# The tail of a batch moved to other slots, VectorE's order in a slot, and where padding rows are zeroed

## The chip, the core and the metric

One core of a Trainium2 chip runs the whole program. The metric is the device time of one execution in microseconds (us). TensorE multiplies matrices into PSUM. VectorE and ScalarE read PSUM and compute, GpSimd computes on SBUF only, and SP (SyncE) issues DMAs. Each engine works through its own queue in order and waits on semaphores that the others raise.

## The reference, cut to what matters

Sixteen sequences (B = 16) of 112 rows and 256 features pass through four layers, each with a residual and a tanh gate:

```python
x = x + tanh(g_xattn[0]) * L0_xattn(layernorm(x), ctx)   # 16 heads of 64, 375 context rows
x = x + tanh(g_ffn[0])   * L0_ffn(layernorm(x))          # fft, one 256x256 product, ifft: one matrix in the end
x = x + tanh(g_xattn[1]) * L1_xattn(layernorm(x), ctx)   # one head of 256
x = x + tanh(g_ffn[1])   * L1_ffn(layernorm(x))          # 16 experts, the best 4 of each row
```

The last layer sends each row to its four best experts out of 16. An expert computes `y = swiglu(t @ w1 + b1) @ w2 + b2`, and the four results are summed with softmax weights.

## The kernel before, in words

**Slots.** Time is cut into slots (`g`). Batch b's attention takes slots 16b to 16b+15, and every engine runs one loop over the slots from -10 to 295. `due(g, at)` gives the batch whose step `at` falls into slot g. Three batches overlap in a slot: the attention of batch b (heads in 8 pairs p: scores S in slot 2p, transposition PT in 2p+3, product O in 2p+4), the first projections of batch b+1 (negative places), and the tail of batch b-1 (places 20 to 45). A period is 16 slots. Below, slots are counted modulo 16.

**Projections.** `KV_AT` lists (kind, number, place): "x" transposes the normed rows, "q", "k" and "v" are the projections, "c" transposes the context, "r" and "e" belong to the router. They share two PSUM banks in turn (`KV`). Use n+2 of a bank waits until ScalarE has copied the high half of use n and VectorE has subtracted it to get the low half. VectorE does that in the slot after (`kv_groups(g - 1)`).

**The tail.** After the first layer's out projection (T0A, step 0) it is a chain through one PSUM bank `TL`: step 1 transposes the normed rows n1, 2 is the fft layer's matrix, 3 transposes n2, 4 makes the query of the second attention (results qk_hi, qk_lo), 5 its scores, 6 transposes prob1, 7 and 8 are the products with context and value matrix, 9 transposes the normed rows tn, 10 is the router. `T_EARLY` and `T_LATE` give the slot of each on TensorE, in front of or behind that slot's projections. Step n waits until the reader of step n-1 is done (`TL_READ`). GpSimd computes the power -0.5 of the variance and VectorE refines it (`refine`, two small steps from SBUF to SBUF).

**Order in a slot.** TensorE: S or PT, early tail step, projections, late tail step, O. VectorE: low halves of the slot before, `tail`, negmax of S, rinv, `ahead` (norm of the next batch: AT_LN, AT_XN), pT_lo, `tail_end`. ScalarE: oT, `tail`, the two exponentials of S or pT_hi, high halves of the projections, `tail_end`. GpSimd: `tail`, the multiplication of prob by rinv, `tail_end`, the scatters.

**Experts.** Each expert has a region of 1920 rows in DRAM (`rows_by_expert`). Slots 41 to 44 of a batch scatter its rows there, one choice each. 72 tiles of 128 rows are then computed: 34 (N_A) planned after batch 13, 22 (N_B) planned after batch 15, and 16 (N_P), one for each expert's last, partly filled tile. The order is A, four of B, the 16 P, the rest of B. SP loads them into six buffers, each with a register load of the start row and a DMA (lines 664 to 674), and waits ahead of tile 34 (k = N_A) until the last batch's rows have landed. Rows behind an expert's last row must be zero, so ScalarE's queue issues 16 DMAs in slots 8 to 38 of batch 0 that write zeros over all 16 regions (1920 KB each). The first scatter waits for them.

Of the kernel before, what the change touches and what calls it, by code (L numbers as in the profile page):

```python
# [272 lines left out]
def program(nc, sb, event, sem, banks, ident, acc, earlier, ones, seen, sel, tile_f, wkv, stage_w, tile_bufs,  # L273
# [5 lines left out]
    with scope:  # L279
# [197 lines left out]
        KV_AT = (("k", 2, 0), ("v", 2, 1), ("k", 3, 3), ("q", 1, 4), ("k", 4, 5), ("v", 3, 6),  # L477
# [53 lines left out]
        AT_SPLIT = (-2, 1, -1, 3)  # L531
# [166 lines left out]
        def _(eng):  # L698
# [40 lines left out]
            def tail(g):  # L739

                tb = due(g, 20)
                if tb:
# [147 lines left out]
        def _(eng):  # L890
# [56 lines left out]
            def tail(g):  # L947

                tb = due(g, 27)
# [121 lines left out]
        def _(eng):  # L1071
# [126 lines left out]
            def tail(g):  # L1198
# [5 lines left out]
                tb = due(g, 23)  # L1204
                if tb:

                    e_tl.wait_ge(eng, tb, 3)
                    e_xb.wait_ge(eng, tb, 1)
                    e_tl_dve.done(eng.scalar_tensor_tensor(x2[:, :], TL[0:TQ, 0:D], gt[0:TQ, 2:3],
                                                           xb1[:, :], ALU.mult, ALU.add))  # L1210
                    e_tl_dve.wait_ge(eng, tb, TL_READ[2][1])
                    stats(ct, x2[:, :], ln_t)
                    e_mv_t.done(eng.tensor_scalar(ln_t[:, 8:9], ln_t[:, 7:8], EPS, None, ALU.add))
                tb = due(g, 27)
                if tb:

                    e_tl.wait_ge(eng, tb, 6)
                    e_tl_dve.done(eng.tensor_reduce(sm1[:, 1:2], TL[0:TQ, 0:SK], AX.X, ALU.max))
                    e_tl_dve.wait_ge(eng, tb, TL_READ[5][1])
                    ct(eng.tensor_tensor(sm1[:, 2:3], sm1[:, 1:2], sm1[:, 0:1], ALU.add))  # L1220
                    ct.wait_ge()
                    e_bias1.done(eng.tensor_tensor(sm1[:, 3:4], sm1[:, 0:1], sm1[:, 2:3],
                                                   ALU.subtract))
                tb = due(g, 31)
                if tb:
# [11 lines left out]
                                                ALU.subtract, ALU.mult))  # L1237

            def tail_end(g):
# [17 lines left out]
                if tb:
# [652 lines left out]
```

## Time and profile before

| | |
|---|---|
| median of 3 runs | 1160.99 us (1158.84 to 1163.97) |
| profiled execution | 1161.57 us, span from first to last instruction 1159.8 us, mean granted clock 0.984 |
| TensorE matmul | 1075.9 us busy, 93% |
| VectorE, ScalarE, GpSimd | 773.1 us (67%), 631.4 us (54%), 519.8 us (45%) |
| DMA | 95.82 MB, of which the 16 zero fills are 30.7 MB |
| chain that ended last | TensorE 61%, VectorE 16%, ScalarE 10% of the span |

Busy shares are means over the whole span. The stages differ: the first batch (to about 90 us) has loads and set-up, from 134 us on the periods are alike, from about 915 us the last tail and the expert tiles run, and after 1120 us the results are gathered. In rows TensorE is PE (its weight loads PEld), VectorE is DVE, ScalarE is ACT, GpSimd is POOL. A start time is counted from the span's start; a matmul's end is modelled and overlaps the next one's start.

### The profile page before, as it was taken

The numbers are of one execution on the slowest core, as the hardware profiler recorded it, in microseconds if no ns is written. First come the engines' busy times: TensorE is split into PE (matmuls) and PEld (weight loads), VectorE is DVE, ScalarE is ACT, GpSimd is POOL, SyncE is SP. The second block draws the span as 40 slices with busy tenths as digits, with TensorE's granted clock in tenths as the row PEclk, the third lists the DMA queues.
The fourth block names the chain that finished last, engine by engine and source line by source line (L and its number), as shares of the span: only waits on it lengthen the run. The fifth ranks groups of instructions, "written<-read, shape, count | busy, mean of one in ns | idle before, by whom it ended". The sixth has DMA issues, their size and how long they took to land.

```text
span 1159.8 us, 22342 instructions
## 1 busy us (share of the span) xinstructions
PE 1075.9 (93%) x7361; PEld 930.8 (80%) x7361; DVE 773.1 (67%) x1963; ACT 631.4 (54%) x1676; POOL 519.8 (45%) x745
## 2 busy tenths in 40 slices
PE   3889999999999999999999999999999779899995
PEld 3688888888888888888788888888887668789983
DVE  2544677767676767776676777676766665686665
ACT  2533556555656565655556565656564545555650
POOL 3512345453535454454535354536354404565441
PEclk9989999999999999999999999999999888999998
DMA  5395882010101011010001010101000522234469
GB/s 150 96 329 207 309 297 63 5 34 9 30 27 31 27 31 35 23 35 22 23 16 32 8 38 9 31 9 31 5 18 9 176 83 78 99 108 152 133 198 287
DMA packets 82382, 95.82 MB, mean 83 GB/s; under 512 B 9291, under 2 KB 74445, under 8 KB 82272
## 3 DMA queue, kind: packets, MB, share of 16 engines
q1 hardware_dynamic: 41904, 44.94, 13.5%
q10 hardware_dynamic: 31520, 32.51, 7.9%
q0 software_dynamic: 8848, 16.96, 4.2%
q8 instruction: 63, 1.03, 0.4%
q14 instruction: 47, 0.39, 0.1%
HBM read 41.98 MB, written 52.39 MB: 81 GB/s over the span
## 4 chain that ended last, share of the span: by engine, by line
PE 61%; DVE 16%; ACT 10%; issue 6%; DMA 4%; POOL 3%; SPq 1%; DVEq 0%; ACTq 0%; POOLq 0%
PE ps_kv L1568 14%; PE ps_ot L1854 8%; PE ps_ot L1668 5%; PE ps_kv L1650 5%; PE ps_s L1811 5%; PE ps_pt L1821 5%; ACT prob L938 4%; DVE negmax L1467 3%; PE ps_pt L1780 3%; PE ps_ot L1793 3%; DVE pT_lo L1478 2%; DVE k_lo L1152 2%; ACT v_hi L928 2%; DMA zb<-places 2%; PE ps_ot L1712 2%
## 5 line engine op out<-in xcount | busy, mean ns | idle before, releaser
L855 POOL TENSOR_TENSOR prob<-prob,rinv 112x750 f32<-112x750 f32 x128 | 185.4, 1448 | 310.7 <-DVE rinv L1472 310.4
L938 ACT ACTIVATE prob<-ps_s,negmax 112x375 f32<-112x375 f32 x256 | 144.7, 570 | 236.4 <-DVE negmax L1467 236.4
L1478 DVE TENSOR_TENSOR pT_lo<-ps_pt,pT_hi 125x672 fp32r<-125x672 f32 x128 | 109.7, 857 | 77.0 <-ACT pT_hi L1051 77.0
L1568 PE MATMUL ps_kv<-ctxT_hi,wkv 128*128 128x376 f32 x512 | 141.6, 357 | 7.8 <-DVE v_lo L1156 3.8
L1467 DVE TENSOR_REDUCE negmax<-ps_s 112x2 f32<-112x750 f32 x128 | 119.0, 930 | 0.1
L1156 DVE TENSOR_TENSOR v_lo<-ps_kv,v_hi 125x512 fp32r<-125x512 f32 x96 | 66.4, 692 | 77.2 <-ACT v_hi L928 77.2
L1568 PE MATMUL ps_kv<-wkv,ctxT_hi 128*125 128x512 f32 x384 | 112.2, 414 | 3.6 <-DVE n_e L1116 2.3
L1821 PE MATMUL ps_pt<-ident,prob 112*125 112x112 f32 x768 | 104.9, 273 | 1.3 <-POOL prob L855 1.3
L814 POOL DMA_INDIRECT places<-ysb,place_i x72 | 70.3, 976 | 69.1 <-ACT ysb L1010 55.9
L1051 ACT ACTIVATE pT_hi<-ps_pt 125x672 fp32r<-125x672 f32 x128 | 93.5, 730 | 9.0 <-PE ps_pt L1821 1.0
L1821 PEld LDWEIGHTS ps_pt<-ident,prob 112*125 112x125 f32 x768 | 95.1, 191 | 1.7 <-POOL prob L855 1.7
L1568 PEld LDWEIGHTS ps_kv<-ctxT_hi,wkv 128*128 128x128 f32 x512 | 85.8, 191 | 11.0 <-ACT xnT L911 6.0
L1039 ACT ACTIVATE oT<-ps_ot 64x112 f32<-64x112 f32 x256 | 65.9, 257 | 51.8 <-PE ps_ot L1854 48.6
L1152 DVE TENSOR_TENSOR k_lo<-ps_kv,k_hi 128x376 fp32r<-128x376 f32 x128 | 69.6, 544 | 30.9 <-ACT k_hi L926 30.2
L1568 PEld LDWEIGHTS ps_kv<-wkv,ctxT_hi 128*125 128x125 f32 x384 | 66.4, 187 | 25.6 <-issue 10.0
L1428 DVE TENSOR_TENSOR tT_lo<-ps_s,tT_hi 128x512 fp32r<-128x512 f32 (+1 forms) x76 | 50.3, 662 | 47.9 <-ACT tT_hi L998 47.8
L1854 PE MATMUL ps_ot<-pT_hi,v_hi 125*128 125x224 f32 x384 | 72.6, 298 | 3.1 <-issue 3.0
L928 ACT ACTIVATE v_hi<-ps_kv 125x512 fp32r<-125x512 f32 x96 | 57.4, 598 | 32.3 <-PE ps_kv L1568 32.3
L926 ACT ACTIVATE k_hi<-ps_kv 128x376 fp32r<-128x376 f32 x128 | 61.9, 484 | 20.9 <-PE ps_kv L1568 20.7
L792 POOL DMA_INDIRECT entries<-entry,at x64 | 61.5, 962 | 18.9 <-issue 14.6
L796 POOL DMA_INDIRECT rows_by_expert<-row,at x64 | 60.1, 940 | 19.5 <-issue 19.2
L1854 PEld LDWEIGHTS ps_ot<-pT_hi,v_hi 125*128 125x128 f32 x384 | 58.0, 193 | 12.9 <-issue 9.7
(298 smaller groups left out, 2623.8 us busy)
## 6 DMA issues: line engine op xcount, KB each, us to landing
rows_by_expert<-stage_w ACTq DMA_DIRECT2D x16, 1920.0 KB, 7.3
xg<-rows_by_expert SPq DMA_DIRECT2D x72, 128.0 KB, 2.1
zb<-places SPq DMA_DIRECT2D x16, 448.0 KB, 15.0
arena<-in_L_ffn_mlp_w SPq DMA_DIRECT2D x24, 256.0 KB, 4.4
ctx_in<-in_ctx SPq DMA_DIRECT2D x16, 375.0 KB
acc<-in_L_xattn_w_kv SPq DMA_DIRECT2D x4, 512.0 KB, 13.1
stage_w<-in_L_ffn_mlp_w SPq DMA_DIRECT2D x8, 256.0 KB, 3.0
x_in<-in_x SPq DMA_DIRECT2D x16, 112.0 KB, 2.1
```

The lines of the kernel that those rows point to most:

```text
L814: eng.indirect_dma_start(places[:, :], bass.IndirectOffsetOnAxis(place_i[:, n:n + 1], 0), ysb[:, j % YB, :], None).then_inc(f_z[j % YB], 16)
L855: e_prob.done(eng.tensor_tensor(prob[0:TQ, p % 2, :, :], prob[0:TQ, p % 2, :, :], rinv[:, 2 * p:2 * p + 2].unsqueeze(2).broadcast_to([TQ, ...
L928: ins = eng.activation(v_hi[0:KEYT, n % NKEY, n // NKEY * 512:(n // NKEY + 1) * 512], bank[0:KEYT, :], ACT.Copy)
L938: e_exp.done(eng.activation(prob[0:TQ, p % 2, half, :], S[0:TQ, half, 0:SK], ACT.Exp, bias=negmax[:, h:h + 1], accum_out=rowsum[:, h:h + 1]))
L1051: e_pt_hi.done(eng.activation(pT_hi[:, :, :, :].rearrange("p h k t -> p h (k t)"), PT[0:KEYT, :, 0:NKEY * TQ], ACT.Copy))
L1152: ins = eng.tensor_tensor(k_lo[:, n, :], bank[:, 0:SKE], k_hi[:, n, :].bitcast(F32), ALU.subtract)
L1156: ins = eng.tensor_tensor(v_lo[0:KEYT, n % NKEY, at], bank[0:KEYT, :], v_hi[0:KEYT, n % NKEY, at].bitcast(F32), ALU.subtract)
L1467: e_max.done(eng.tensor_reduce(negmax[:, 2 * p:2 * p + 2], S[0:TQ, :, 0:SK], AX.X, ALU.max, negate=True))
L1478: e_pt_lo.done(eng.tensor_tensor(pT_lo[:, :, :, :].rearrange("p h k t -> p h (k t)"), PT[0:KEYT, :, 0:NKEY * TQ], pT_hi[:, :, :, :].bitcas ...
L1568: last = eng.matmul(out_, lhs(i, k), rhs(j, k), start=(n == 1), stop=(n == KT * len(PASSES)))
L1821: last = eng.transpose(PT[0:KEYT, half, k * TQ:(k + 1) * TQ], prob[0:TQ, p % 2, half, k * KEYT:(k + 1) * KEYT], ident[0:TQ, 0:TQ])
L1854: last = eng.matmul(OT[:, 0:2 * TQ].rearrange("p (h t) -> p h t", t=TQ), vv[i][0:KEYT, k, p * 128:(p + 1) * 128], pT[j][:, :, k, :], start ...
```

## The change

Three things are changed.

1. Places. The tail's steps 1 to 5 move from the end of slots 21, 22, 24, 25, 26 to the front of 22, 23, 25, 26, 27; steps 6 and 7 from the front of 28 and 29 to their end. The steps of the other engines follow. Of the projections, k2 goes from slot 0 to 1, v2 from 1 to 2, q1 from 4 to 5 (behind k4), q0 of the next batch from 14 to 11, c1 from 13 to 12, k0 from 14 to 13, k1 from 15 to 14. AT_XN goes from slot 7 to 9.
2. VectorE calls `tail` behind negmax, rinv and `ahead` instead of ahead of them. x2 and the second attention's maximum move from `tail` to `tail_end`, n2 moves from `tail_end` of slot 23 to `tail` of 24, and the router's ranking moves to `tail` (places 34 and 35). On GpSimd xb1 moves behind the multiplication. A projection two uses behind an "r" now waits for VectorE's half of it too.
3. Padding. The 16 zero fills and the waits for them go. VectorE's plan of batch 15 computes each expert's first row behind its last (`pad_i`), and SP, behind the loads of tiles 30 to 33, copies 128 zero rows to there from a spare tile in DRAM, four experts behind each load. The load of tile 38 waits for all of them.

```diff
-        KV_AT = (("k", 2, 0), ("v", 2, 1), ("k", 3, 3), ("q", 1, 4), ("k", 4, 5), ("v", 3, 6),
+        KV_AT = (("k", 2, 1), ("v", 2, 2), ("k", 3, 3), ("k", 4, 5), ("q", 1, 5), ("v", 3, 6),
                  ("k", 5, 7), ("v", 4, 8), ("k", 6, 9), ("v", 5, 10), ("k", 7, 11), ("x", 0, -6),
-                 ("c", 0, -4), ("c", 1, -3), ("q", 0, -2), ("k", 0, -2), ("k", 1, -1), ("v", 0, -1),
+                 ("q", 0, -5), ("c", 0, -4), ("c", 1, -4), ("k", 0, -3), ("k", 1, -2), ("v", 0, -1),
                  ("v", 1, 0), ("r", 0, 36), ("e", 0, 38))
...
-        AT_LN, AT_XN, AT_XB0 = -10, -9, 6
-        T_EARLY = {20: 0, 28: 6, 29: 7, 30: 8, 32: 9, 33: 10}
-        T_LATE = {21: 1, 22: 2, 24: 3, 25: 4, 26: 5}
+        AT_LN, AT_XN, AT_XB0 = -10, -7, 6
+        T_EARLY = {20: 0, 22: 1, 23: 2, 25: 3, 26: 4, 27: 5, 30: 8, 32: 9, 33: 10}
+        T_LATE = {28: 6, 29: 7}
...
-        AT_SPLIT = (-2, 1, -1, 3)
+        AT_SPLIT = (-3, 1, -1, 3)
...
+        PAD_AT = tuple(range(N_A - 4, N_A))
...
+                if k == N_A + B_FIRST:
+                    eng.wait_ge(f_zero, 16 * NE)
                 c_turn.wait_ge(eng, k - XB + 1)
...
+                if k in PAD_AT:
+                    eng.wait_ge(s_pad, 1)
+                    first = PAD_AT.index(k) * NE // len(PAD_AT)
+                    for e in range(first, first + NE // len(PAD_AT)):
+                        end = eng.value_load(pad_i[0:1, e:e + 1], min_val=0, max_val=NE * REGION - TILE)
+                        eng.dma_start(rows_by_expert[bass.ds(end, TILE), :],
+                                      rows_by_expert[NONE * TILE:(NONE + 1) * TILE, :]).then_inc(f_zero, 16)
...
-                if g in AT_ZERO:
-
-                    if g == AT_ZERO[0]:
-                        eng.wait_ge(s_fill, 2)
-                    e = AT_ZERO.index(g)
-                    eng.dma_start(rows_by_expert[e * REGION:(e + 1) * REGION, :].rearrange("(p n) d -> p n d", p=128),
-                                  zeros.unsqueeze(1).broadcast_to([128, REGION // 128, D])).then_inc(f_zero, 16)
...
+                    if not early:
+                        ct(eng.tensor_tensor(todo[:, :], n_e[:, :], region[:, :], ALU.add))
+                        ct.wait_ge()
+                        eng.tensor_copy(pad_i[:, :], todo[:, :]).then_inc(s_pad, 1)
...
                 for step, kind, n in kv_groups(g - 1):
                     projection(step, kind, n)
-                tail(g)
...
                 ahead(g)
+                tail(g)
...
-                    if KV_ORDER[use - 2][0] not in "xr" or kind == "w":
+                    if KV_ORDER[use - 2][0] != "x":
                         eng.wait_ge(kv_dve, KV_LO[use - 1])
```

## Rows read from the trace of the kernel before

**Rows 1.** stages; columns: time, us, busy PE, PEld, DVE, ACT, POOL, clock, DMA, GB/s

```profile
134.20:188.91 54.71, 53.84 (x367) 45.74 (x367) 38.66 (x101) 31.63 (x89) 22.75 (x27) 1.00 0.68 237
790.76:845.47 54.71, 53.72 (x367) 45.68 (x367) 38.65 (x101) 31.53 (x89) 26.59 (x32) 1.00 0.07 19
```

**Rows 2.** timeline of PEld: start, us, line, operation, [idle before <- releaser]

```profile
574.89 0.41 PEld L1854 LDWEIGHTS ps_ot<-pT_hi,v_hi 125*128 125x128 f32 x3 [0.42 <-issue]
616.48 0.20 PEld L1687 LDWEIGHTS ps_ot<-ident,n12t 112*128 112x128 f32 x2 [0.87 <-issue]
619.71 0.47 PEld L1695 LDWEIGHTS ps_ot<-qbk,nT 128*112 128x112 f32 x4 [0.42 <-ACT nT L944]
626.59 0.30 PEld L1568 LDWEIGHTS ps_kv<-ctxT_hi,wkv 128*128 128x128 f32 x2 [0.35 <-ACT xnT L911]
```

**Rows 3.** timeline of DVE, slots 7 and 8

```profile
614.58 0.63 DVE L1170 SCALAR_TENSOR_TENSOR ln_t<-ln_t 112x1 f32<-112x1 f32 x1
616.74 0.93 DVE L1467 TENSOR_REDUCE negmax<-ps_s 112x2 f32<-112x750 f32 x1
```

**Rows 4.** timeline of ACT, slot 8

```profile
617.70 0.57 ACT L938 ACTIVATE prob<-ps_s,negmax 112x375 f32<-112x375 f32 x1 [3.42 <-DVE negmax L1467]
```

**Rows 5.** timeline of PE, slots 10 and 11: x, O, PT

```profile
623.38 0.36 PE L1603 MATMUL ps_kv<-ident,xn 112*128 112x112 f32 x2
624.61 0.49 PE L1854 MATMUL ps_ot<-pT_hi,v_hi 125*128 125x224 f32 x3
625.61 0.81 PE L1821 MATMUL ps_pt<-ident,prob 112*125 112x112 f32 x6
```

**Rows 6.** timeline of ACT, slots 9 and 10

```profile
621.29 0.60 ACT L989 ACTIVATE qk_hi<-ps_ot,kbq 128x112 fp32r<-128x112 f32 x2
625.56 0.79 ACT L911 ACTIVATE xnT<-ps_kv,cols 128x112 f32<-128x112 f32 x2
```

**Rows 7.** timeline of DVE, slot 9

```profile
622.07 0.57 DVE L1262 SCALAR_TENSOR_TENSOR qk_lo<-ps_ot,kbq,qk_hi 128x112 fp32r<-128x112 f32 x2
```

**Rows 8.** timeline of POOL, slot 7

```profile
613.66 1.54 POOL L855 TENSOR_TENSOR prob<-prob,rinv 112x750 f32<-112x750 f32 x1
```

**Rows 9.** timeline of all engines, batch 0, slot 7

```profile
51.65 1.44 POOL L855 TENSOR_TENSOR prob<-prob,rinv 112x750 f32<-112x750 f32 x1 [0.26 <-DVE rinv L1472]
51.72 1.38 DVE L1172 SCALAR_TENSOR_TENSOR ln_h<-ln_h 112x1 f32<-112x1 f32 x1
```

**Rows 10.** timeline of all engines, slot 12

```profile
573.11 0.42 PE L1811 MATMUL ps_s<-k_hi,q_hi 64*112 64x376 f32 x2
577.85 0.55 DVE L1143 TENSOR_TENSOR ctxT_lo<-ps_kv,ctxT_hi 128x375 fp32r<-128x375 f32 x1 [1.47 <-ACT ctxT_hi L920]
```

**Rows 11.** timeline of PE, head

```profile
16.28 3.72 PE L1650 MATMUL ps_kv<-xnT,wq 128*128 128x112 f32 x16 [0.24 <-DVE ctxT_lo L1143]
69.14 0.54 PE L1643 MATMUL ps_kv<-ident,ctx_in 125*128 125x125 f32 x3 [1.45 <-DMA ctx_in<-in_ctx]
```

**Rows 12.** stages of the head, columns as in rows 1

```profile
70.00:75.00 5.00, 5.00 (x28) 4.95 (x28) 1.74 (x10) 0.84 (x3) 0.00 (x1) 0.55 0.98 350
75.00:80.00 5.00, 5.00 (x35) 4.42 (x34) 2.16 (x3) 2.11 (x6) 1.43 (x1) 0.76 0.75 260
```

**Rows 13.** timeline of SP's DMA issues, tiles 33, 34 and 41

```profile
1030.28 0.34 SPq L674 DMA_DIRECT2D xg<-rows_by_expert  x1
...
1044.24 0.34 SPq L674 DMA_DIRECT2D xg<-rows_by_expert  x1
...
1052.46 0.34 SPq L674 DMA_DIRECT2D xg<-rows_by_expert  x1
```

**Rows 14.** timeline of DVE, first step of the last plan

```profile
1026.02 0.42 DVE L1341 TENSOR_REDUCE full<-cmp_b 112x16 f32<-112x256 f32 x1
```

**Rows 15.** timeline of PE, tile 34

```profile
1046.33 0.44 PE L1767 MATMUL ps_s<-ident,xg 128*128 128x128 f32 x2 [1.52 <-DMA xg<-rows_by_expert]
```

More of the change, by code:

```diff
@@ L744, in tail @@
                     e_rs_t.done(eng.tensor_tensor(ln_t[:, 9:10], ln_t[:, 8:9], consts[0:TQ, 0:1], ALU.pow))
-                    e_xb.done(eng.tensor_tensor(xb1[:, :], x1[:, :], rows[0:TQ, 1, :], ALU.add))
-                tb = due(g, 23)
+                tb = due(g, 24)
                 if tb:
@@ L756, in tail_end @@
             def tail_end(g):
-                tb = due(g, 23)
+                tb = due(g, 21)
+                if tb:
+                    e_xb.done(eng.tensor_tensor(xb1[:, :], x1[:, :], rows[0:TQ, 1, :], ALU.add))
+                tb = due(g, 24)
                 if tb:
@@ L977, in tail_end @@
             def tail_end(g):
-                tb = due(g, 21)
+                tb = due(g, 22)
                 if tb:
                     normed(tb, 1)
-                tb = due(g, 24)
+                tb = due(g, 25)
                 if tb:
                     normed(tb, 3)
-                tb = due(g, 25)
+                tb = due(g, 26)
                 if tb:
@@ L1203, in tail @@
                     normed(tb, 0)
-                tb = due(g, 23)
+                tb = due(g, 24)
                 if tb:
[L1207 to L1223, printed above, removed]
+                    e_rs_t.wait_ge(eng, tb, 2)
+                    normed(tb, 1)
                 tb = due(g, 31)
@@ L1237, in tail @@
                                                 ALU.subtract, ALU.mult))
+                tb = due(g, 34)
+                if tb:
+                    ct.wait_ge()
+                    ct(eng.tensor_tensor(cmp_b[:, :, :], cmp_b[:, :, :], earlier[0:TQ, :, :], ALU.mult))
+                    ct.wait_ge()
+                    ct(eng.tensor_tensor(cmp_a[:, :, :], cmp_a[:, :, :], cmp_b[:, :, :], ALU.add))
+                    ct.wait_ge()
+                    ct(eng.tensor_reduce(rk[:, 0, :], cmp_a[:, :, :], AX.X, ALU.add))
+                    ct.wait_ge()
+                    e_seen.wait_ge(eng, tb, 0)
+                    e_mask.done(eng.tensor_scalar(mask[:, :], rk[:, 0, :], TOPK - 0.5, None, ALU.is_lt))
+                tb = due(g, 35)
+                if tb:
+                    e_gexp.wait_ge(eng, tb, 1)
+                    ct(eng.scalar_tensor_tensor(rk[:, 3, :], rk[:, 0, :], TOPK - 0.5, rk[:, 1, :],
+                                                ALU.is_lt, ALU.mult, accum_out=rs[:, 1:2]))
+                    ct.wait_ge()
+                    ct(eng.reciprocal(rs[:, 2:3], rs[:, 1:2]))
+                    ct.wait_ge()
+                    e_route.done(eng.tensor_scalar(route[:, :], rk[:, 3, :], rs[:, 2:3],
+                                                   gt[0:TQ, 3:4], ALU.mult, ALU.mult))
             def tail_end(g):
@@ L1253, in tail_end @@
                 if tb:
-                    e_rs_t.wait_ge(eng, tb, 2)
-                    normed(tb, 1)
-                tb = due(g, 25)
+                    e_tl.wait_ge(eng, tb, 3)
+                    e_xb.wait_ge(eng, tb, 1)
+                    e_tl_dve.done(eng.scalar_tensor_tensor(x2[:, :], TL[0:TQ, 0:D], gt[0:TQ, 2:3],
+                                                           xb1[:, :], ALU.mult, ALU.add))
+                    e_tl_dve.wait_ge(eng, tb, TL_READ[2][1])
+                    stats(ct, x2[:, :], ln_t)
+                    e_mv_t.done(eng.tensor_scalar(ln_t[:, 8:9], ln_t[:, 7:8], EPS, None, ALU.add))
+                tb = due(g, 26)
                 if tb:
@@ L1265, in tail_end @@
                     e_tl_dve.done(last)
+                tb = due(g, 27)
+                if tb:
+                    e_tl.wait_ge(eng, tb, 6)
+                    e_tl_dve.done(eng.tensor_reduce(sm1[:, 1:2], TL[0:TQ, 0:SK], AX.X, ALU.max))
+                    e_tl_dve.wait_ge(eng, tb, TL_READ[5][1])
+                    ct(eng.tensor_tensor(sm1[:, 2:3], sm1[:, 1:2], sm1[:, 0:1], ALU.add))
+                    ct.wait_ge()
+                    e_bias1.done(eng.tensor_tensor(sm1[:, 3:4], sm1[:, 0:1], sm1[:, 2:3],
+                                                   ALU.subtract))
                 tb = due(g, 28)
```

37 lines of the change are left out of this document (9 added, 28 removed).

## The prediction

> **What bounds the kernel now.** I read the stage table first. The steady stretch, in which one batch's attention, the batch before's tail and the next batch's first projections share 16 slots, takes 54.71 us a batch with TensorE busy 53.7 at clock 1.00. It takes that both while the zero fill moves 237 GB/s and when only 19 GB/s flow [rows 1]. So TensorE's queue is the bound there, and the zero fill already costs nothing after batch 1. What an order change can win is TensorE's waits. The weight-load row, which shows the start of each group of matmuls, has four real ones in a period: the O product on pT_lo (0.42), tail step 3 on n2 (0.87), step 4 on the copy nT (0.42), k7 on v5's low half and xnT (0.35) [rows 2]. Then I followed VectorE, ScalarE and GpSimd through slots 7 to 12, since those waits come from there: slots 7 to 9 hold nearly all of VectorE's small tail work, so negmax of slot 8 starts at 616.74 and ScalarE's exponentials have waited 3.42 us for it [rows 3, 4].
>
> Fourteen periods (batches 1 to 14) carry tail and next batch together, so 1 us a period is 14 us. The profiled execution took 1161.57 us, 0.6 above the median of the runs, and the sum is made against it.
>
> **The spread, part by part.** By my count of PE work, the fullest slots of before (4, 0 and 14) lose q and k projections to slots 5, 11, 13 and 14. The work is the same; only waits can change.
>
> *What goes.* Step 3 moves from the end of slot 8 to the front of slot 9, and n2 now comes before the choice block and after a negmax that is earlier: its 0.87 goes. k7 stands behind step 5 in slot 11, so v5's low half has time: 0.35 goes. The second-layer exponential moves from slot 11 to slot 12 on ScalarE, so pT_hi of slot 11 no longer queues behind it: 0.42 goes. Step 4 still follows step 3 by one ScalarE copy that queues behind the exponentials: its 0.42 stays. Gone: 0.87 + 0.42 + 0.35 = 1.6 us a period.
>
> *What comes, slot 11.* Step 4 now runs in slot 10 ahead of v5 and x, and ScalarE takes its result (qk_hi) only after the exponentials of slot 10, v5's copy and the two xnT copies; VectorE's qk_lo follows, and step 5 stands in TensorE's queue right behind O and PT. In before, x started at 623.38 on TensorE and xnT ended at 625.56 + 0.79 = 626.35, 2.97 later, because the exponentials had waited for a late negmax [rows 5, 6]. With that lag, step 5 could start 2.97 + qk_hi 0.60 + qk_lo 0.57 + about 0.3 of handoffs = 4.4 us after x; TensorE's own work until then is x 0.12 (to the next start), O 1.00 and PT 0.58 = 1.7 [rows 5 to 7]. Upper bound of the wait 2.7. Lower bound, with ScalarE idle when x ends: the later of v_hi and xnT leaves about 1.1, then 0.60, 0.57 and 0.3, against 1.6 of work: 0.95. Between them the state of VectorE decides. In slot 9 it now has rinv, then the refinement for xn, then pT_lo, then k6's low half and the negmax of slot 10. rinv releases GpSimd's 1.44 us multiply of prob, and the refinement reads two SBUF tensors: at 51.72 exactly this sequence held the second refinement step for 1.38 us, until 53.10, where GpSimd's multiply from 51.65 ended (53.09); at 614.58 a step held 0.63, to the end of the multiply of 613.66 [rows 3, 8, 9]. In before's steady slot 7 the xn refinement escaped, because GpSimd first did a small power there. In slot 9 there is none. So negmax of slot 10 comes about 3.4 us behind its S, ScalarE's exponentials end about when x has been done for a microsecond, and the wait comes out near 2.2. I take 2.2, by the row at 51.72, which is the same instruction sequence.
>
> The Trainium skill (SBUF — State Buffer, Who interferes with whom) states that a VectorE instruction with two SBUF inputs and a GpSimd instruction that reads SBUF exclude each other, and that the later one blocks for the whole of the other. The trace agrees in the 1.38 us above.
>
> *What comes, slots 12 and 13.* c0 and c1 stand together in slot 12 and k0 in slot 13, where before they had slots 12, 13 and the end of 14. c1 needs the bank that q0 (end of slot 11) leaves, and k0 needs c1's low half. ScalarE copies c only after the exponentials of slot 12. In before S of slot 12 started at 573.11 and c0's low half ended at 577.85 + 0.55 = 578.40, 5.3 us later [rows 10]; a second c adds about 0.45. TensorE's own work from S to k0 is now S 0.69, two c 0.82, step 6 0.42, O 1.02 and PT 0.58 = 3.5 (start-to-start distances of the same period). With before's lag, the wait is 5.75 - 3.5 = 2.2. VectorE is less behind here (q0's low half, then negmax at once): S to negmax 1.4 with q0 in front, negmax 0.96, exponentials 1.11, two copies 0.8, low half and handoffs 0.9 = 5.1: wait 1.6. With negmax prompt it is 0.6 less and c1's own bank wait is still there: 1.0, or 0.6 if that falls too. I take 1.6, bounds 0.6 and 2.2.
>
> Sum: 2.2 + 1.6 - 1.6 = +2.2 us a period, 14 x 2.2 = **+31 us**. Bounds: 0.95 + 0.6 - 1.6 = 0 and 2.7 + 2.2 - 1.6 = +3.3, so 0 to +46.
>
> **VectorE's order in a slot** puts negmax ahead of the tail; that is inside the above (slot 8's negmax about 1.4 us earlier). **TensorE's extra wait** for VectorE's half of r sits before q1 in slot 5, behind k4; VectorE does r's 0.17 first in its slot, so S's and PT's 1.3 us cover it; uncovered it is 0.2 a period. Cost 0.
>
> **Head.** At the start q0 (3.72 us there) goes ahead of both c, and xn is two slots later in program order only. k0 must wait for c, which waited for q0: bounds 0 and +3.7, taken +2, since TensorE waits elsewhere in the first slots [rows 11]. Without the zero fill the batch-1 context load need not share 350 GB/s: TensorE waited 1.45 us for it, and then its granted clock was 0.55 in 70 to 75 us and 0.76 in 75 to 80, means between the levels 1.2 GHz (0.5) and 2.4 GHz (1.0), which is 2.2 + 1.2 us of full-speed work [rows 11, 12]. Bounds 0 and -4.9; taken -3. Head together **-1**.
>
> **Padding.** 16 copies now stand in SP's queue between the loads of tiles 30 to 33 and tile 34, each a register load and a DMA. SP's loads ran 7 steps in 8.22 us when nothing held them, 1.17 each [rows 13]. They may begin when VectorE's first plan step is done, 1026.02 + 0.42 + about 0.5 = 1027.0 [rows 14]. Sixteen copies, three loads and tile 34's own then end at about 1028 + 19 x 1.12 to 1.17 = 1049 to 1050. Before, tile 34 was issued at 1044.24, held by the last scatter, and TensorE waited for it to 1046.33 [rows 13, 15]; after it the tiles follow back to back, so nothing behind it gives time back. Tile 33 (1030.28 before) goes to about 1044 and is late too, inside the same delay. Cost **+5**. Bounds: 0 (SP does not mind, or the scatter ends later), +9 (0.2 more per copy, and loads landing behind copies of the same queue). The wait for all copies at tile 38 comes four loads later and is covered by six buffers.
>
> **The rest.** Two VectorE steps in the plan, about 0.4 us; ScalarE's 16 DMA issues go, and ScalarE is no bound. The last batch's tail alone runs steps up to one slot later, while the scatter stays in slots 41 to 44: 0, give or take 3.
>
> Total 1161.6 + 31 - 1 + 5 = 1196.6; less the 0.6 by which the profiled run lies above the median: **1196**.
>
> **Rivals.** (a) *VectorE's reductions first pay, faster.* Place: ScalarE's queue in slots 10 and 12. If negmax is prompt enough that the two new waits stay under 1.6 - 4/14 = 1.3 us together, the change wins; with none at all it wins 1.6 x 14 = 22: 1161 - 22 + 4 = 1143. For it: the 3.42 us that ScalarE waited. Against: even an idle ScalarE leaves 0.95 + 0.6. Chance 0.06. (b) *The gate in slot 9 stays open*: GpSimd starts late, xn is not held; step 5 waits 1.0, so +1.0 a period, +14 + 4: 1179. Chance 0.22. (c) *Every such VectorE step behind rinv is held.* In slot 5 the refinement for n1 now meets the multiply and the xb1 add that was moved behind it, and in slot 15 the third step before tn; pT_lo and k4's low half in slot 5 come up to 2 us later, and v3 in slot 6 waits 0.4 to 1.1: 14 x 0.75 = 10 more, 1206. By the skill's rule above it is this. Chance 0.15. (d) *New waits equal the old*, with the copies hidden or the head's gain paying for them: 1158 to 1165. Chance 0.07. My forecast, 1186 to 1203, has 0.50.
>
> **From these the numbers.** A measurement here can tell 0.5% (5.8 us). Faster 0.06, same 0.07, slower 0.87. The range leaves out (a), (d) and the top of (c): 1170 to 1212.
>
> **What would show it.** Period: 56.5 to 57.5 between the same slot of two batches (55.7 under b, 53.1 under a). TensorE's row: the 0.87 before step 3 gone, some 2 us before step 5's first matmul with qk_lo as releaser, some 1.2 before k0 with the low half of c. VectorE: the xn refinement of 1.3 us or so in each period. SP: 16 DMA issues about 1.1 us apart and tile 34 at 1049. Clock 1.00 in 70 to 80 us. I am wrong if step 5 or k0 start without a wait, or if SP issues the copies in much less.

## The result and the profile after

The changed kernel takes 1233.54 us (median of 4 runs, 1233.13 to 1236.98) where the kernel before takes 1162.48 beside it: a ratio of 1.062, 95% interval 1.059 to 1.066. It is slower, by 71 us and not by the 35 that were forecast (31 - 1 + 5), and beyond the upper end of the forecast, 1212. The profiled execution took 1233.86 us with a span of 1232.0 and a mean granted clock of 0.960.

Where the 72.3 us between the two profiled executions arise, by four marks that both traces have (the first transposition of xn of batch 2 and of the last batch, the plan step `full` of the last plan, tile 34's load):

| stretch | before | after | more |
|---|---|---|---|
| start to x of batch 2 | 130.97 | 138.25 | 7.3 |
| 13 periods, to x of the last batch | 711.25 | 755.23 | 44.0 |
| last period and last tail, to `full` | 183.80 | 199.20 | 15.4 |
| `full` to tile 34's load | 18.22 | 26.23 | 8.0 |
| rest | | | -2.4 |

A second pair of traces, x1 and x2 below, gives 8.0, 44.1, 7.7, 8.4 and 1.4 by the same marks. The last tail's 15.4 and the rest do not repeat, the other three do.

The timeline of TensorE after, at the new place of step 5 in slot 11 (the three products onto `ps_ot`), and k7 behind it (`ps_kv`), in two batches that follow each other. Columns: start, us, engine, line, operation, [idle before <- releaser].

```profile
488.02 0.36 PE L1614 MATMUL ps_kv<-ident,xn 112*128 112x112 f32 x2
...
545.26 0.36 PE L1614 MATMUL ps_kv<-ident,xn 112*128 112x112 f32 x2
...
549.31 0.76 PE L1579 MATMUL ps_ot<-ctxT_hi,qk_hi 128*112 128x376 f32 x2 [2.03 <-DVE qk_lo L1279]
...
551.12 0.83 PE L1579 MATMUL ps_kv<-ctxT_hi,wkv 128*128 128x376 f32 x2
551.75 0.83 PE L1579 MATMUL ps_kv<-ctxT_lo,wkv 128*128 128x376 f32 x2
...
604.08 0.36 PE L1614 MATMUL ps_kv<-ident,xn 112*128 112x112 f32 x2
...
608.12 0.58 PE L1579 MATMUL ps_ot<-ctxT_hi,qk_hi 128*112 128x376 f32 x2 [2.02 <-DVE qk_lo L1279]
...
609.22 0.51 PE L1579 MATMUL ps_kv<-ctxT_hi,wkv 128*128 128x376 f32 x2
609.56 0.50 PE L1579 MATMUL ps_kv<-ctxT_lo,wkv 128*128 128x376 f32 x2
```

Both batches wait 2.0 us for qk_lo, as forecast. Behind the wait the same pairs of products start 0.63 us apart in the first batch and 0.34 in the second. The stages of these stretches (time, us, busy PE, PEld, DVE, ACT, POOL, clock, DMA, GB/s) say why:

```profile
549.30:551.20 1.90, 1.89 (x7) 1.85 (x8) 1.29 (x3) 0.26 (x1) 1.28 (x1) 0.56 0.00 0
551.20:553.10 1.90, 1.90 (x9) 1.90 (x8) 0.87 (x3) 0.00 (x0) 1.44 (x3) 0.54 0.01 0
...
608.00:610.00 2.00, 1.89 (x11) 1.92 (x12) 1.94 (x4) 0.37 (x1) 1.27 (x1) 1.00 0.00 0
610.00:612.00 2.00, 2.00 (x19) 2.00 (x17) 0.88 (x3) 0.48 (x1) 1.54 (x3) 1.00 0.01 0
```

In the first batch TensorE's granted clock is at 1.2 GHz (0.5; the slices take in a bit of either side) for step 5 and k7, in the next it stays at 2.4 GHz. So periods of 57.25 and 58.80 us take turns through the whole steady stretch (x at 488.02, 545.26, 604.08), against 54.71 [rows 1]. The 2.0 us come from where the forecast had them. VectorE, GpSimd and ScalarE after, slots 9 and 10, and VectorE in slot 5:

```profile
541.52 1.44 POOL L866 TENSOR_TENSOR prob<-prob,rinv 112x750 f32<-112x750 f32 x1 [2.71 <-DVE rinv L1482]
541.59 1.38 DVE L1176 SCALAR_TENSOR_TENSOR ln_h<-ln_h 112x1 f32<-112x1 f32 x1
544.60 0.92 DVE L1477 TENSOR_REDUCE negmax<-ps_s 112x2 f32<-112x750 f32 x1
545.55 0.57 ACT L949 ACTIVATE prob<-ps_s,negmax 112x375 f32<-112x375 f32 x1 [3.13 <-DVE negmax L1477]
547.80 0.62 ACT L1000 ACTIVATE qk_hi<-ps_ot,kbq 128x112 fp32r<-128x112 f32 x2
548.60 0.57 DVE L1279 SCALAR_TENSOR_TENSOR qk_lo<-ps_ot,kbq,qk_hi 128x112 fp32r<-128x112 f32 x2
...
585.41 1.38 DVE L1174 SCALAR_TENSOR_TENSOR ln_t<-ln_t 112x1 f32<-112x1 f32 x1 [0.19 <-POOL ln_t L754]
```

The refinement's second step for xn lasts 1.38 us, to 542.97, where GpSimd's multiply ends (542.96), exactly as in [rows 9]. The median of its 16 executions is 1380 ns. negmax of slot 10 then starts 2.2 us behind the end of S, ScalarE idles 3.13 us, and qk_hi stands behind all of it. The other waits, on TensorE and its weight loads (PEld): step 4, c0, c1, k0, step 3 and the projection v3:

```profile
542.48 0.47 PEld L1706 LDWEIGHTS ps_ot<-qbk,nT 128*112 128x112 f32 x4 [0.45 <-ACT nT L955]
...
555.53 0.31 PEld L1654 LDWEIGHTS ps_kv<-ident,ctx_in 125*128 125x128 f32 x3 [0.25 <-issue]
556.37 0.51 PE L1654 MATMUL ps_kv<-ident,ctx_in 125*128 125x125 f32 x3 [0.29 <-DVE q_lo L1151]
559.86 0.62 PE L1579 MATMUL ps_kv<-ctxT_hi,wkv 128*128 128x376 f32 x2 [1.00 <-DVE ctxT_lo L1147]
...
588.76 0.20 PEld L1698 LDWEIGHTS ps_ot<-ident,n12t 112*128 112x128 f32 x2 [0.26 <-issue]
589.26 0.75 PEld L1579 LDWEIGHTS ps_kv<-wkv,ctxT_hi 128*125 128x125 f32 x4 [0.30 <-issue]
```

Step 3's 0.87 of [rows 2] has become 0.26, k7's 0.35 and O's 0.42 are gone, step 4's stays. Last, the plan step on VectorE and SP's issues behind it (L676 loads a tile, L683 is a zero copy, four in a group):

```profile
1092.68 0.42 DVE L1347 TENSOR_REDUCE full<-cmp_b 112x16 f32<-112x256 f32 x1
1094.33 4.61 SPq L683 DMA_DIRECT2D rows_by_expert<-rows_by_expert  x4
1099.69 0.35 SPq L676 DMA_DIRECT2D xg<-rows_by_expert  x1
...
1112.47 0.35 SPq L676 DMA_DIRECT2D xg<-rows_by_expert  x1
1113.64 4.43 SPq L683 DMA_DIRECT2D rows_by_expert<-rows_by_expert  x4
1118.91 1.48 SPq L676 DMA_DIRECT2D xg<-rows_by_expert  x2
...
1121.03 0.44 PE L1778 MATMUL ps_s<-ident,xg 128*128 128x128 f32 x2 [1.94 <-DMA xg<-rows_by_expert]
```

Four copies and a load take 6.4 us (1112.47 to 1118.91), 1.3 a DMA, and TensorE stands 1.94 us for tile 34.

### The profile page after: what moved, and what is told of

The parts are those of the page before. It is cut to its first block and busy times, and to the rows that moved or that the text cites. A ratio compares the mean times of both kernels' runs of the same rounds, so it can differ in the third digit from the quotient of the medians.

```text
span 1232.0 us, 22439 instructions
## 1 busy us (share of the span) xinstructions
PE 1102.4 (89%) x7361; PEld 958.5 (78%) x7361; DVE 833.2 (68%) x1965; ACT 627.7 (51%) x1676; POOL 518.6 (42%) x745
## 3 DMA queue, kind: packets, MB, share of 16 engines
q10 hardware_dynamic: 544, 1.05, 0.3%
## 5 line engine op out<-in xcount | busy, mean ns | idle before, releaser
L1579 PE MATMUL ps_kv<-ctxT_hi,wkv 128*128 128x376 f32 x512 | 149.4, 375 | 18.6 <-DVE ctxT_lo L1147 17.7
L1579 PE MATMUL ps_kv<-wkv,ctxT_hi 128*125 128x512 f32 x384 | 115.4, 423 | 6.2 <-DVE wkv L1459 2.8
L1579 PEld LDWEIGHTS ps_kv<-ctxT_hi,wkv 128*128 128x128 f32 x512 | 94.6, 202 | 23.9 <-DVE ctxT_lo L1147 20.5
L1865 PE MATMUL ps_ot<-pT_hi,v_hi 125*128 125x224 f32 x384 | 69.7, 291 | 2.1 <-DVE pT_lo L1489 2.1
L1579 PE MATMUL ps_kv<-ctxT_lo,wkv 128*128 128x376 f32 x256 | 68.3, 350 | 0.0
L1661 PEld LDWEIGHTS ps_kv<-xnT,wq 128*128 128x128 f32 x512 | 65.7, 202 | 2.6 <-ACT xnT L922 2.6
```

What stands on the lines that cost most here:

```text
L1579: last = eng.matmul(out_, lhs(i, k), rhs(j, k), start=(n == 1), stop=(n == KT * len(PASSES)))
L1661: last = eng.matmul(bank[:, a * TQ:(a + 1) * TQ], wq[:, k, p * 128:(p + 1) * 128], xnT[:, k, :], start=(k == 0), stop=(k == KT - 1))
L1865: last = eng.matmul(OT[:, 0:2 * TQ].rearrange("p (h t) -> p h t", t=TQ), vv[i][0:KEYT, k, p * 128:(p + 1) * 128], pT[j][:, :, k, :], start ...
```

## The experiments

Times are medians. A ratio is to the kernel before beside the run, 1162.6 us for u1 to u4 and 1163.5 for u5 to u8. Differences from the changed kernel are to its 1233.5 above.

**u1: the hold.** VectorE's `ahead` in front of rinv:

```diff
+                ahead(g)
+                for p in range(NP):
                     st = due(g, AT_S[p] + 1)     # rinv
...
-                ahead(g)
                 tail(g)
```

> The changed kernel, with VectorE's `ahead` (the refinement for xn) moved in front of rinv in each slot, nothing else. Theory H (GpSimd's multiply, released by rinv, holds the refinement for 1.38 us, so the negmax of slot 10 and all behind it come late): the refinement takes its plain 0.16, negmax of slot 10 comes 1.4 us earlier, the wait before step 5 falls from 2.0 to about 0.8, and the half-rate stretch behind it goes too (0.78 a period on average). 14 x (1.2 + 0.78) = 28 less: 1205 us. Rival (ScalarE's own chain, v5's copy, xnT, qk_hi, sets step 5, whatever VectorE does): the wait stays above 1.6 and the time at 1225 to 1233.

Measured: 1200.07 us, ratio 1.032 (1.030 to 1.035). VectorE in slots 9 and 10 and TensorE at step 5:

```profile
524.29 0.16 DVE L1176 SCALAR_TENSOR_TENSOR ln_h<-ln_h 112x1 f32<-112x1 f32 x1
526.10 0.93 DVE L1477 TENSOR_REDUCE negmax<-ps_s 112x2 f32<-112x750 f32 x1
...
530.88 0.57 PE L1580 MATMUL ps_ot<-ctxT_hi,qk_hi 128*112 128x376 f32 x2 [0.83 <-DVE qk_lo L1279]
```

The step takes 0.16, the wait 0.83, every period 56.05 to 56.09, and none has a slow stretch. Moving three small instructions (the two of the refinement and xn) past one is worth 33 us. Theory H holds.

**u2: step 5 behind k7 and q0.**

```diff
-        T_LATE = {28: 6, 29: 7}
+        T_LATE = {27: 5, 28: 6, 29: 7}
...
                 for at in T_EARLY:
                     tb = due(g, at)
-                    if tb:
+                    if tb and (at != 27 or tb.off >= B - 2):
...
                 for at in T_LATE:
                     tb = due(g, at)
-                    if tb:
+                    if tb and (at != 27 or tb.off < B - 2):
```

> The changed kernel, with step 5 behind slot 11's projections k7 and q0 (except for the tails of the last two batches). Theory A (step 5 is only too early in TensorE's queue): 1.1 us of k7 and 1.9 of q0 cover its wait; wait and half-rate stretch go, 13 x 2.8 = 36 less: about 1197 us. Rival B (the whole slot is late): k7 needs the bank of v5, whose low half VectorE computes behind qk_lo and which ended at 549.76, after step 5 had started; then k7 takes over the wait, 2.0 to 2.5 us, with the half-rate stretch behind it, and the time stays at 1230 to 1242.

Measured: 1272.61 us, ratio 1.096 (1.091 to 1.101), worse than both expected. k7 after this edit, in TensorE's timeline, and then the stage behind it:

```profile
567.46 0.96 PE L1579 MATMUL ps_kv<-ctxT_hi,wkv 128*128 128x376 f32 x2 [2.62 <-DVE v_lo L1160]
```

```profile
568.00:570.00 2.00, 2.00 (x9) 2.00 (x8) 0.14 (x1) 0.29 (x1) 1.84 (x2) 0.50 0.00 0
```

Rival B is right about the mechanism: the whole slot is late, and k7 takes the wait over. It is longer (2.62), and the clock now falls in every period of the middle (61.4 us each), for k7 and all of q0. That was not in the 1242.

**u3 and u5: does the wait bring the clock down?** Products with unused results are put into the wait, 15 and then 10:

```diff
+                st = due(g, AT_S[5] + 1)
+                if st and due(g, 27):
+                    e_exp.wait_ge(eng, st, 12)
+                    for _ in range(15):             # u5: 10
+                        eng.matmul(S[0:TQ, 0, 384:496], ident[0:TQ, 0:TQ], ident[0:TQ, 0:TQ], start=True, stop=True)
                 for at in T_EARLY:
```

> The changed kernel with 15 products of the identity with itself (112 columns each, about 0.12 us each, results unused) put into the 2.0 us wait before step 5. Theory C (the wait is what takes TensorE's clock down to 1.2 GHz in every second period, at 1.55 us each): the granted clock stays 1.00 behind step 5, every period takes 57.25, 7 x 1.55 = 11 less although there is more work: 1222 us. Rival (the clock falls by itself every 116 us or for the load as a whole): periods alternate as before, 1233 us, or more if the products delay step 5.

> As u3_filler, with 10 products instead of 15. In u3_filler each took two instructions and 15 of them 2.88 us, 0.85 more than the wait, so that every period took 57.97, none of them with a half-rate stretch. Ten take 1.92 us and fit into the wait. Theory C (the wait brings the clock down): every period 57.25, and 7 x 1.55 = 11 less than the changed kernel, 1222 us. Rival (the products only bought their own excess): periods of 57.3 and 58.8 by turns, 1233 us.

Measured: u3 1236.67 us (ratio 1.063, 1.058 to 1.067), u5 1221.93 (1.050, 1.047 to 1.054). u3 looks like the rival, but its periods are all 57.95 to 57.98: no alternation, and 0.7 of excess filler in each. In u5 they are 57.24 to 57.32. u5's slot 11, TensorE's timeline and then the stages:

```profile
539.49 2.13 PE L1840 MATMUL ps_s<-ident 112*112 112x112 f32 x20
541.67 0.57 PE L1579 MATMUL ps_ot<-ctxT_hi,qk_hi 128*112 128x376 f32 x2
```

```profile
541.30:543.20 1.90, 1.84 (x13) 1.69 (x12) 1.88 (x5) 0.63 (x1) 0.92 (x1) 1.00 0.01 2
543.20:545.10 1.90, 1.90 (x17) 1.90 (x16) 1.17 (x4) 0.48 (x1) 1.49 (x2) 1.00 0.00 0
```

TensorE does more work and the kernel is 11.6 us faster than the changed one: the half rate came from standing still. Theory C holds, with its size (1222).

**u4: the padding.** The old zero fills and waits come back into the changed kernel, the `if k in PAD_AT` block on SP and `pad_i` go.

> The changed kernel with the old padding (16 zero fills of whole regions on ScalarE's queue, the first scatter waits for them; none on SP). By the trace (16 copies at about 1.3 us each on SP ahead of tile 34): tile 34's load comes 7.6 us sooner after the plan, 1226 us. By the prediction's terms (copies +5, zero fill -3 in the head): 2 less, 1231 us. Rival (tile 34 is late for another reason, and only the head feels the zero fill): 1233 to 1238 us.

Measured: 1222.80 us, ratio 1.051 (1.047 to 1.056), so the new padding costs 10.7 (8.8 between the two profiled executions, and 7.9 of these behind `full`: 131.4 us to the end instead of 139.3). x of batch 2 starts at 137.63 instead of 138.25: in this order of work the zero fill makes no difference to the head, so the prediction's gain there is not to be had. The rival is out. (The 16 zero fills are 31.5 MB, not the 30.7 of the table above: queue q10, which carries them, moves 32.51 MB before and 1.05 MB in v4.)

**u6: c1 and k0 back in slots 13 and 14**, on top of u1:

```diff
-                 ("q", 0, -5), ("c", 0, -4), ("c", 1, -4), ("k", 0, -3), ("k", 1, -2), ("v", 0, -1),
+                 ("q", 0, -5), ("c", 0, -4), ("c", 1, -3), ("k", 0, -2), ("k", 1, -2), ("v", 0, -1),
```

> u1_xn_before_rinv with c1 back in slot 13 and k0 back in slot 14 (ahead of k1), where they were before. Theory K (c1 and k0 stand too close behind the context's copies): their waits of 0.30 and 1.00 us go, 14 x 1.3 = 18 less than u1's 1200: 1182 us. Rival (the waits move on to k1 or to S of slot 16, since ScalarE and VectorE have as much to do as before): 1195 to 1202 us.

Measured: 1197.40 us, ratio 1.030 (1.027 to 1.034), 2.7 less than u1. From TensorE's waits in 440 to 870 us (line <- releaser: us, times, longest):

```profile
PE ps_ot L1724 <- ACT prob1T L968: 6.8, 7, 1.0
```

k0's wait is gone and step 7 has one of the same length: in slot 13 only c1 (0.5 us) stands in front of it now, where k0 stood. The rival holds in time and kind, though the wait moved to step 7 and not to k1 or S.

**u7: the head.** Slots -6 to -1 of batch 0 in the old order, and the first weight split in slot -2:

```diff
+            head = (("x", 0, -6), ("c", 0, -4), ("c", 1, -3), ("q", 0, -2), ("k", 0, -2), ("k", 1, -1), ("v", 0, -1))
-            own = [(due(slot, at), kind, n) for kind, n, at in KV_AT]
+            own = [(due(slot, at), kind, n) for kind, n, at in (KV_AT if slot >= 0 else head)]
```

> The changed kernel, with batch 0's own first projections (slots -6 to -1) in the old order c0, c1, q0, k0, k1, v0 and the first weight split in slot -2; from slot 0 on as changed. Theory L (q0 ahead of c in the first batch, when nothing else covers the copies of c, makes k0 and all behind it late, and this is the head's whole loss): x of batch 2 starts at about 131 instead of 138.25, 7 less: 1226 us. The prediction's term for it was 2 us: 1231. Rival (the loss comes from the other places, k2 and v2 one slot later, in batch 0's slots 0 to 15): 1233.

Measured: 1226.56 us, ratio 1.054 (1.051 to 1.058): 7.0 less. x of batch 2 starts at 132.98, 5.3 earlier and not 7, so theory L holds for 5.3 of the head's 7.3; the 2.0 that are left could be the rival's. In the changed kernel's head TensorE waits 3.69 for c's low half before k0, 2.78 for a weight half before v0, 2.08 and 2.27 in the first O and PT, and its clock falls in 50 to 60 us (0.77) as well as in 80 to 90 (0.66). Which of these carries how much was not separated.

**u8: qk_hi in front of the exponentials**, on top of u1: ScalarE's block for place 26 moves from `tail_end` to `tail`.

> u1_xn_before_rinv with ScalarE's qk_hi taken in front of slot 10's exponentials instead of behind v5's and xn's copies. Theory Q (step 5 waits for its place in ScalarE's queue, not for work): ScalarE is idle there while it waits for negmax, step 5's remaining 0.83 us goes: 14 x 0.83 = 12 less than u1's 1200, 1188 us. Rival (the exponentials start late behind it, and c1, k0 or O wait that much more): 1197 to 1206 us.

Measured: 1182.64 us, ratio 1.017 (1.014 to 1.021), 17.4 less than u1, more than theory Q's 12. Periods are 55.0; TensorE's waits in 440 to 870 us are these two:

```profile
PE ps_kv L1580 <- DVE ctxT_lo L1147: 8.0, 8, 1.0
PE ps_kv L1655 <- DVE q_lo L1151: 2.3, 8, 0.3
```

**The last runs**, v and w, ran where the kernel before takes 1200 us (1199.6 beside v1 to v4, 1200.3 beside w1 to w4), so only their ratios compare. x1, the kernel before again, and x2 ran where it takes 1161. So x1 gave no trace of the 1200, and what made the difference is open. v4's trace shows one part of it, in slot 13 from 190 us on: ScalarE stands 1.97 us, though the product it copies (PE, L1719) is over at 584.1:

```profile
582.62 1.50 PE L1719 MATMUL ps_ot<-prob1T,ctx_in 125*128 125x112 f32 x12
586.10 0.36 ACT L971 ACTIVATE nT<-ps_ot 128x224 f32<-128x224 f32 x1 [1.97 <-remote]
```

Its periods are 56.1 with matmuls as busy as in [rows 1] (53.75) and the clock at 1.00. In v1, v2, w1 and w2 ScalarE has such gaps of up to 1.6, 1.7, 2.3 and 1.5 us at other places of the steady stretch. v3, w3 and w4 have none there, but some of up to 3.8, 5.0 and 3.8 us in the last tail and the expert tiles. The twelve traces from the other places have no ScalarE gap with this releaser at all. Behind `full`, too, all eight runs are some 10 us longer than there, whatever the kernel: 141 to 146 us to the end with the old fills (v2, v3, w1, w4) against 130 to 134 (before, x1, u4), and 152 to 153 with the new padding (v1, v4, w2, w3) against 139 to 144. Since the gaps do not lie alike in all kernels, a ratio here may favour one kernel over another.

**v1, v2, w1, w2: all that was found, together.** u8 with c ahead of q0; v1 and v2 have c0, c1 in slot 12, w1 and w2 c1 in slot 13 with q0; v2 and w1 have the old zero fills:

```diff
-                 ("q", 0, -5), ("c", 0, -4), ("c", 1, -4), ("k", 0, -3), ("k", 1, -2), ("v", 0, -1),
+                 ("c", 0, -4), ("c", 1, -4), ("q", 0, -3), ("k", 0, -2), ("k", 1, -1), ("v", 0, -1),   # w: c1 at -3
```

> u8_qk_hi_early (xn in front of rinv, qk_hi in front of the exponentials) with the next batch's first projections as c0, c1 in slot 12, q0 in 13, k0 in 14, k1 and v0 in 15, and the first weight split in slot -2; so the head too has c ahead of q0. The new padding stays. Theory (the waits of c1 and k0 and the head's q0 are the rest of the loss outside the padding; 1.9 us of q0 in slot 13 cover the copies of c and prob1T's, which took over in u6): 14 x 1.3 = 18 and 5 in the head less than u8's 1183: 1160 us. Rival (a new wait takes their place, as in u6): 1172 to 1180.

> v1_all_waits with the old zero fills instead of the copies on SP's queue. By u4 against the changed kernel (10.7 us): 1150 us if v1 takes 1160, which is below the kernel before (1162). Rival (tile 34 is no longer what the end waits for when the rest is earlier): as v1.

> The changed kernel with all that the runs point to: xn in front of rinv, qk_hi in front of the exponentials, c0 in slot 12, c1 and q0 in 13, k0 in 14, k1 and v0 in 15, and the old zero fills. Theory (the waits named were the loss, and the change's gone waits of 1.6 us a period are a real gain): a period of about 54.0, 0.7 less than before's 54.70; 14 x 0.7 = 10 less, some 5 more in the last tail: 1157 us where the kernel before takes 1162, a ratio of 0.995. Rival (a new wait takes their place): a period of 55 or more and a ratio over 1.005.

> w1_c1_13_old_fill with the new padding (copies on SP's queue, no zero fills). By u4 and v2: 8 to 11 more than w1, a ratio to the kernel before of 1.003 to 1.005. Rival (the copies are hidden once the rest is early): as w1.

Measured: v1 1202.50 us, ratio 1.002 (1.000 to 1.005); v2 1194.23, 0.994 (0.992 to 0.996); w1 1193.54, 0.994 (0.992 to 0.996); w2 1201.18, 1.001 (0.998 to 1.003). v1's theory asked for 0.998 and v2's for 0.990; the rivals (1.008 and more for v1, no difference for v2) are out. So with the waits taken out and the old fills, the new places are 0.6% faster there than the kernel before, and the new padding takes it back (8.3 and 7.6 us). How much of the 0.6% is left where the kernel before takes 1161 was not measured. The period ahead of ScalarE's gaps is 54.51 to 54.54 in all four runs against 54.70 before [rows 1] (54.68 in v4): 14 x 0.17 = 2 us, or 0.2%, is an estimate from these. w1 doesn't reach the period of 54.0: 54.54 before the gaps begin, 55.15 after (56.6 to 56.9 in three). In w2's waits in 406 to 850 us the next one stands in line:

```profile
PE ps_ot L1719 <- ACT prob L970: 7.3, 8, 0.9
```

Step 6 now waits 0.9 for the second layer's exponential. The rival is half right.

**v4: the new padding alone**, put into the kernel before.

> The kernel before with the new padding alone (no zero fills, 16 copies on SP's queue ahead of tile 34, two more VectorE steps). By the changed kernel's trace (copies at about 1.3 us each, tile 34 8.0 us later behind the plan step) and u4, where the zero fill did not move the head: 8 to 10 more, 1171 us. By the prediction's terms (+5 on SP's queue, -3 in the head, where the context load need not share the DMA engines): 2 more, 1165 us. Rival (nothing changes, since tile 34 waits for the last scatter): 1162.

Measured: 1204.38 us, ratio 1.004 (1.002 to 1.006), 4.8 more, between the two sums. x of batch 2 starts at 126.99 (130.97 in the trace of before): with before's order the head seems to gain without the zero fill, as the prediction had it, though the two traces are of the two kinds of place. Pairs from one place say the same with less: with c ahead of q0, x of batch 2 starts at 130.11 without the fill and 132.77 with it (v1, v2), and at 131.65 and 132.89 (w2, w1), where the same kernel differs by up to 0.9 (before, x1).

**v3 and w4: the order alone; w3: the rest without it.** v3 and w4 are the kernel before with `tail(g)` moved behind `ahead(g)`, w3 is the changed kernel with it moved back.

> The kernel before with one part of the change alone: VectorE calls `tail` behind negmax, rinv and `ahead`; all places as before. Theory O (a maximum taken early lets ScalarE start its exponentials early, and that pays by itself): the 3.42 us of ScalarE's wait in slot 8 shrinks and TensorE's 0.42 and 0.35 go, 14 x 0.5 = 7 less: 1155 us. Rival (x2 of place 23 then waits for rinv, and n2 with it, so step 3's wait of 0.87 grows by a microsecond or more): 14 x 1 = 14 more, 1176 us.

> As v3_order_alone: the kernel before with VectorE's `tail` behind negmax, rinv and `ahead`, nothing else. In v3 every period took 57.4, 2.7 more than before's 54.70 where nothing disturbs it, with 1.4 before step 3 and 0.9 before step 6. If that is the order's own price: 14 x 2.7 = 38 and some 4 in the last tail, 1204 us, a ratio of 1.035. If v3 was only caught by what disturbed the kernel before too: a ratio of 1.01 to 1.02.

> The changed kernel with VectorE's `tail` ahead of negmax again, as before the change; places, the steps in `tail` and `tail_end`, and the padding as changed. Theory (the refinement behind rinv in slot 9 and the queue of ScalarE make the loss, and the order of VectorE's queue in the even slots little): step 5 still waits 2.0, 1228 to 1245 us. Rival (the order costs by itself, since tail steps now wait behind rinv): the wait is gone or halved, 1208 us or less.

Measured: v3 1224.65 us, ratio 1.021 (1.016 to 1.025); w4 1222.36, 1.017 (1.014 to 1.020); w3 1255.48, 1.045 (1.042 to 1.048). TensorE's waits in 406 to 850 us, first w4, then w3:

```profile
PE ps_ot L1687 <- DVE n12t L1195: 11.1, 15, 1.1
PE ps_ot L1707 <- ACT prob L952: 4.6, 8, 0.6
```

```profile
PE ps_ot L1579 <- DVE qk_lo L1279: 9.5, 8, 2.1
PE ps_ot L1706 <- ACT nT L955: 11.2, 8, 1.4
```

The order alone is no gain: step 3 waits up to 1.1 for n2, as the rival said, and step 6 for the exponential. In w3 step 5's wait is up to 2.1 as before, so the order doesn't make it. The ratios add up (1.045 and 1.017 to 1.062), but w3's lies between the two expectations, and with the gaps above the order's share is not settled better than 1 to 3%.

**x1, x2: both kernels unchanged.**

> The kernel before, unchanged, for its trace where it takes 1200 us. Theory (what disturbs these runs is a ScalarE idle that recurs each period, as in v4): periods of 56.1 and a ScalarE idle of 2 us ahead of the copy cT, 13 x 1.4 = 18 of the 38. Rival (TensorE itself is slower there): the same waits as before, but longer matmuls or a lower granted clock.

> The changed kernel, unchanged, beside x1. If the parts add up (w3: places and padding alone 1.045, w4: order alone 1.017): a ratio of 1.06 here as well, 1274 us. If the idle times hit the kernel before harder than the changed one: a ratio of 1.03 to 1.04, 1240 us, and then the order was nothing by itself.

Measured: 1161.10 and 1232.70 us, ratio 1.061 (1.057 to 1.065). The ratio is the one by which the parts add up, and the alternation is the same (57.28 and 58.78).

## Why the prediction was wrong in size

By its own terms, in us; a period's terms count 14 times:

| term | predicted | measured |
|---|---|---|
| wait of step 5 | 2.2 | 2.03 |
| waits of c1 and k0 | 1.6 | 1.29 |
| waits that go | -1.6 | -0.8 net (57.25 - 54.71 - 2.03 - 1.29) |
| half rate behind the wait | not in the sum | 0.8 (1.55 in every second period) |
| 14 periods | 31 | 47 |
| head | -1 | 7.3 |
| copies on SP | 5 | 8.0 |
| last tail | 0 | 12 (15.4 less one period's 3.4); 4 by x1 and x2 |
| rest | 0 | -2.4; 1.4 by x1 and x2 |

*Right:* the bound (TensorE's queue), the chain (refinement held by GpSimd, late negmax, ScalarE's queue, qk_hi, step 5), its length to 0.2 us, k0's wait, and the refinement's 1.38 in each period. By the Trainium skill (SBUF — State Buffer, Who interferes with whom) a VectorE instruction with two SBUF inputs and a GpSimd instruction that reads SBUF exclude each other; the trace agrees here (542.97 and 542.96), and u1 shows that the order of the two decides. Rival (b) is out. Of rival (c) the mechanism is there (the n1 refinement in slot 5 takes 1.38 too, at 585.41), but the projection v3 waits 0.30 behind it, less than the rival's lower price.

*The step that failed first* is that the sum took a wait at its own length and put what TensorE does behind it at nothing. The prediction had read a fall of the clock behind a wait in the head [rows 12] and didn't ask it of the 2.2 us that it forecast itself. That is 11 us, by u5. A 0.83 us wait (u1) brought no fall, 2.0 one in every second period, 2.62 one in every period of the middle (u2). With these 11 us in its sum the forecast would have been 1207, still inside its range; it was the other terms, the head and the last tail above all, that carried the result out of it. Of the 37 us that the forecast missed, 11 are the half rate, 5 the periods' waits together, 8 the head, 3 the copies, 12 the last tail, less 2 of the rest.

*Mis-sized:* the waits that go. The three rows went nearly as said, 0.61 + 0.42 + 0.35 = 1.4 of the 1.6, but the projection v3's 0.30 and c0's 0.25 came, which stood only in a rival or nowhere: another 11 us, less the 7 by which the new waits were shorter.

*The head:* q0 ahead of c was taken at 2 with a bound of 3.7, reading one row. k0's wait is 3.69, but u7 shows 5.3 in the head and 7.0 in the whole: behind it stand the waits for the weight half, O and PT and a clock fall, not priced one by one. The bound was no bound: it held for one wait, not for those behind it. The zero fill's gain in the head, taken at 3, shows as 1.2 to 4.0 with c ahead of q0 (v1, v2; w1, w2; v4) and not in the changed order (u4). The clock was at 1.00 in 70 to 80 us as said, but it had fallen at 50 to 60 and fell at 80 to 90.

*SP:* the cadence was 1.3 and not 1.12 to 1.17, taken from loads into SBUF where the copies go from DRAM to DRAM; within the bounds of 0 to 9.

*The last tail* was put at 0, give or take 3, and is 12 in one pair of traces and 4 in the other. In both changed traces step 5 of the last batch waits 1.95 where it waited for nothing, step 9 (on tn) 3.8 where it waited 2.4, and the step 9 of the batch before 1.62 where it waited 0.28: 4.6 together. In TensorE's timeline, step 9 of the last batch before, then its steps 5 and 9 after:

```profile
993.74 0.38 PE L1687 MATMUL ps_ot<-ident,n12t 112*128 112x112 f32 x2 [2.43 <-DVE n12t L1234]
```

```profile
1033.47 0.56 PE L1579 MATMUL ps_ot<-ctxT_hi,qk_hi 128*112 128x376 f32 x2 [1.95 <-DVE qk_lo L1279]
...
1059.86 0.61 PE L1698 MATMUL ps_ot<-ident,n12t 112*128 112x112 f32 x2 [3.77 <-DVE n12t L1222]
```

The rest changes from one trace of a kernel to the next. From the step 9 of the batch before to this step 5 the changed kernel takes 58.3 us at a mean granted clock of 0.74, in x2 54.7 at 0.84. Why the clock differs there is open.

What the change gains shows only in w1 and v2: 0.6% there, where the undisturbed periods would give 0.2% (the estimate above).

## What to carry to other kernels

Price a TensorE wait of 2 us or more with the matmuls behind it at half rate, and where one can't be removed, unused products in it may pay (11.6 us here). In front of an instruction that releases GpSimd, place VectorE's small SBUF steps, and take a copy where its engine idles, not where the loop happens to have it: the two moves were worth 51 us here and changed no work. Work that is hidden on one queue (the zero fill on ScalarE) is not made cheaper by doing less of it on a queue at whose end everything waits.

## What was not expected of the hardware

The clock's answer to a wait that is the same each time (2.02 and 2.03 us) took turns from period to period, as steadily in x2 as in the first trace; why it does so is open. Filling it with unused products kept it at 1.00. And the kernel before took 1161 to 1163 us in four sets of runs and 1200 in two. What traces show of that difference is ScalarE gaps with their input ready (1.97 us a period in v4, with TensorE's clock and matmuls as ever), in all eight runs from there and in no other, and some 10 us more behind `full`. The cause is open.
